# Latent attention: the reciprocal of the softmax sums is written to its PSUM bank and multiplied from there

## The reference, cut to what matters

```
q = (x @ wq).reshape(B, T, 2, 4, 128)
k_lat, v_lat = x @ wk_down, x @ wv_down          # 2 groups x 32
k, v = k_lat @ wk_up, v_lat @ wv_up
probs = softmax(mask(einsum(q, k) * 128 ** -0.5))
y = einsum(probs, v);  x = x + y @ wo
```

## Time and profile before

| what | value |
|---|---|
| time, median of 3 runs | 1840.62 us (1838.76 to 1849.7) |
| the profiled execution | 1839.44 us, of it 1837.3 us from the first to the last instruction |
| granted TensorE clock, mean | 0.911 of full speed |
| latent attention with GpSimd's additions | 1391 to 1745 us |
| the eight reciprocals, L1588 | 26.9 us |
| the eight multiplications, L1590 | 21.6 us |

### The profile page before, as it was taken

One profiled execution on the slowest core, in us unless ns is written; L12 is line 12 of the kernel. 1 busy time (PEld: TensorE's weight loads), 2 busy tenths in 40 slices (PEclk: granted clock), 3 DMA queues, 4 the chain that ended last, 5 costly groups with the idle time before them and its releaser, 6 DMA issues.

```text
span 1837.3 us, 25913 instructions
## 1 busy us (share of the span) xinstructions
PE 1579.0 (86%) x8863; PEld 801.0 (44%) x8863; DVE 1162.2 (63%) x2315; ACT 787.1 (43%) x1031; POOL 802.8 (44%) x987
## 2 busy tenths in 40 slices
PE   4666599869999999999699959998968978898779
PEld 2222366533334333343266636776634333333256
DVE  5888632489878788786243243334268988887841
ACT  2232233263565565556533324444443333444443
POOL 1223663645464636463636363500002546667900
PEclk9788599986999999999889979998988988999979
DMA  5000000141102002000000000000043000000000
GB/s 146 1 0 0 1 1 0 46 117 32 28 2 54 2 5 51 2 3 2 1 1 1 0 0 1 0 0 1 0 137 96 23 23 1 1 1 1 1 6 17
DMA packets 39123, 36.88 MB, mean 20 GB/s; under 512 B 10191, under 2 KB 36272, under 8 KB 38899
## 3 DMA queue, kind: packets, MB, share of 16 engines
q1 hardware_dynamic: 36826, 28.48, 5.5%
q10 hardware_dynamic: 2136, 7.10, 1.8%
q0 software_dynamic: 64, 0.00, 0.0%
HBM read 26.10 MB, written 8.91 MB: 19 GB/s over the span
## 4 chain that ended last, share of the span: by engine, by line
PE 68%; DVE 14%; issue 3%; ACT 3%; POOL 2%; DMA 1%; SPq 0%; DVEq 0%; POOLq 0%; ACTq 0%
PE PS L1374 11%; PE PS L948 10%; PE PS L1322 10%; PE PS L1393 10%; PE PS L936 9%; PE PS L1822 3%; PE PS L1840 3%; DVE sb_rope_mp L1558 3%; POOL sb_H L1480 2%; DVE sb_latent_mp L1558 2%; DVE sb_latent_rec L1588 1%; DVE sb_H L227 1%; PE PS L1834 1%; PE PS L941 1%; PE PS L1351 1%
## 5 line engine op out<-in xcount | busy, mean ns | idle before, releaser
L1558 DVE TENSOR_REDUCE sb_rope_mp<-PS 128x1 f32<-128x512 f32 (+3 forms) x560 | 344.3, 667 | 65.1 <-PE PS L1326 31.3
L1435 ACT ACTIVATE sb_rope_PT<-PS 128x1024 f32<-128x1024 f32 (+3 forms) x320 | 273.4, 895 | 203.8 <-PE PS L1378 104.3
L1000 DVE SCALAR_TENSOR_TENSOR sb_X<-PS,sb_gates,sb_X 128x128 f32 (+1 forms) x320 | 90.1, 344 | 241.2 <-PE PS L948 241.2
L1322 PE MATMUL PS<-sb_rope_K,sb_rope_Q 96*128 96x512 bf16 (+3 forms) x640 | 212.5, 372 | 11.7 <-ACT sb_rope_V L1420 9.6
L581 POOL TENSOR_SCALAR sb_pbelow<-sb_pa,sb_ptrial 128x512 f32<-128x512 f32 x124 | 196.8, 1597 | 6.4
L1558 DVE TENSOR_REDUCE sb_latent_mp<-PS 128x1 f32<-128x512 f32 (+2 forms) x280 | 175.5, 668 | 36.6 <-PE PS L1322 26.7
L588 POOL TENSOR_TENSOR sb_pbelow<-sb_pbelow 128x1024 f32<-128x1024 f32 (+1 forms) x248 | 182.0, 734 | 19.6
L936 PE MATMUL PS<-sb_HT,sb_w 128*128 (+1 forms) x384 | 182.0, 611 | 3.9 <-DVE sb_seed L519 2.3
L1374 PE MATMUL PS<-sb_rope_Q,sb_rope_K 99*128 99x512 bf16 (+3 forms) x640 | 179.4, 352 | 1.4 <-ACT sb_rope_PT L1435 0.9
L1374 PE MATMUL PS<-sb_latent_Q,sb_latent_K 96*128 96x512 bf16 (+7 forms) x640 | 158.8, 369 | 5.4 <-ACT sb_w0b L1435 2.4
L977 ACT ACTIVATE sb_moe_hidden<-PS,sb_vec 128x512 f32<-128x512 f32 x128 | 87.7, 687 | 159.8 <-PE PS L936 155.6
(11 more groups left out here) (315 smaller groups left out, 2716.9 us busy)
## 6 DMA issues: line engine op xcount, KB each, us to landing
sb_latent_Q<-latent_parts SPq DMA_DIRECT2D x48, 128.0 KB, 2.8
sb_rope_Q<-rope_parts ACTq DMA_DIRECT2D x9, 384.0 KB
rope_parts<-sb_rope_parts SPq DMA_DIRECT2D x24, 128.0 KB, 2.4
latent_parts<-sb_latent_parts SPq DMA_DIRECT2D x12, 256.0 KB, 2.6
sb_rope_tab<-in_rotation SPq DMA_DIRECT2D x1, 2048.0 KB, 8.2
sb_rope_K<-rope_parts ACTq DMA_DIRECT2D x6, 256.0 KB
latent_parts<-sb_latent_parts SPq DMA_DIRECT2D x12, 128.0 KB, 2.5
sb_latent_K<-latent_parts SPq DMA_DIRECT2D x48, 32.0 KB, 2.2
```

What stands on the lines that cost most here:

```text
L1000: ins = v.scalar_tensor_tensor(xi, k.PS[:, 4 + b:5 + b, i * P:(i + 1) * P], gate, xi, ALU.mult, ALU.add)
L1322: ins = pe.matmul(k.PS[:, bank, at:at + w], self.Q[0:self.rows, g % 2, j, 0, q0:q0 + P], self.K[0:self.rows, g % 2, j % self.kheads, 0, kc ...
L1435: s.activation(self.PT[u % self.B][:, 2 * p:2 * p + 2, q0:CH], k.PS[:, 2 * p:2 * p + 2, q0:CH], ACT.Exp, scale=self.scale).then_inc(self.e ...
L1558: v.tensor_reduce(self.mp[:, n % 2, kc, heads[0]:heads[-1] + 1, i], k.PS[:, bank, 0:len(heads) * w].rearrange("p (h k) -> p h k", h=len(he ...
```

## The change

Of the branch for `summed`, the reciprocal now writes to the PSUM bank it reads, and the multiplication reads the reciprocal there. Both are followed by a wait for their own end (`ch`). `normed` and `free` are raised by two separate semaphore instructions after the multiplication; before, `free` was raised by the reciprocal itself and `normed` by the multiplication. The tile `rec` isn't used in this stage any more. The additions of GpSimd and of DVE stay as they are.

```diff
                 v.wait_ge(self.moved, n + 1)
-                v.reciprocal(self.rec[:, :], k.bank(bank)).then_inc(free, 1)
-                v.wait_ge(free, uses + 1)
-                v.tensor_tensor(self.On[:, n % 2, :], self.O[:, n % 2, :], self.rec[:, :], ALU.mult) \
-                    .then_inc(self.normed, 1)
+                ch(v.reciprocal(k.bank(bank), k.bank(bank)))
+                ch(v.tensor_tensor(self.On[:, n % 2, :], self.O[:, n % 2, :], k.bank(bank), ALU.mult))
+                v.sem_inc(self.normed, 1)
+                v.sem_inc(free, 1)
             else:
                 ch(v.tensor_tensor(self.On[:, n % 2, :], self.O[:, n % 2, :], k.bank(bank), ALU.mult))
```

## The result

The changed kernel took 1835.03 us (median of 19 runs, 1823.63 to 1847.3), the kernel before, measured again with it, 1848.49 us (19 runs, 1837.35 to 1853.99). The ratio is 0.9931, with a 95% interval of 0.9909 to 0.9953: 12.8 us less, 8.7 to 16.8. The forecast was 19.5 us less, 1821 us, in a range from 1810 to 1832. The median lies above the range; the direction was right, the gain two thirds of the one forecast, and the kernel before itself measured 8 us above the 1840.62 that the forecast was taken from. Both differences are followed up here. Taken as a gain, 12.8 us does lie in what the range allows (8.6 to 30.6 us under 1840.6), at its low end.

A forecast was written before the change was run, and what follows sets the result against it. PE bound the chain (68%), waiting for a ring bank while L1590 waited for GpSimd. DVE's 17.4 us in chunks 1 to 5 plus 2.2 in chunks 6 and 7 made 19.6, taken as 19.5: 1840.6 - 19.5 = 1821 us, range 1810 to 1832.

The forecast's parts named there:

- What stretched the multiplication, and what a PSUM operand does: L1590: with two SBUF inputs it waits for GpSimd's addition; reading PSUM, 0.686 us each, DVE's sum 16.1 us less.
- The reciprocal's bound of 0.04 us: Reciprocal writing PSUM: no change expected, bounded by 0.04 us either way, 0.3 us for eight.
- Bookkeeping and the held bank: Behind each multiplication: separate semaphores cost 0.25 us; bank freed 0.94 us later, without starving DVE in chunks 1 to 6.
- The chain, 12.3 us in chunks 1 to 5: PE's waits at the sums: 17.0 us of "issue" become 5 x 0.94 = 4.7, 12.3 us gained.
- What is late next: DVE's additions L1480 behind the sums wait for GpSimd likewise, leaving DVE 1.75 us ahead per chunk, not 2.8.
- the 17.4 us: DVE's side of chunks 1 to 5: 5 x 1.75 plus 8.6 us of its idle time at low clock.
- The clock, 8 us: TensorE behind five sums: low clock falls from 33.7 to 17 us, each worth half; 8 us gained.
- Chunk 6, 2.3 us: Copy L1478 done earlier, POOL's next addition sooner: 2.5 us gained, less 0.2 for one more collision.
- the additions inherit the wait: Rival: DVE becomes the bound through its additions waiting for GpSimd; 11 us gained, 1829.6 us; chance 0.10.
- the clock falls as before: Rival: pauses of a microsecond suffice for low clock; only the chain's 14.5 us gained, 1826 us; chance 0.18.
- Slower by over 1%: Whole kernel: would need 2.3 us more per chunk, called twice what the other side costs; chance 0.02.
- the other side: Rival: multiplication still waits for GpSimd and the bank is passed on late; 4 us slower, 1844.6 us; chance 0.05.

The follow-up runs named there:

- e1: Kernel before, with the bank held until the multiplication's end and both semaphores raised separately, reciprocal still to SBUF: stage 348.7 us, before 352.0.
- e4: Changed kernel, but the multiplication itself raises the bank's semaphore and PE and ACT wait for that instead of `normed`: stage 332.4 us, changed kernel 338.6.
- e2: Kernel before, with VectorE's second-unit addition in chunks 2 to 7 replaced by a maximum with one SBUF input: stage 352.2 us, before 352.0.
- e3: Changed kernel, with VectorE's second-unit addition in chunks 2 to 7 replaced by a maximum with one SBUF input: stage 331.7 us, changed kernel 338.6.
- e11: Changed kernel, with the negated maxima kept in the last maximum's PSUM bank for the split, in both causal attentions: stage 332.5 us, ratio 0.9864 to before.
- e7: Changed kernel, with TensorE's pauses behind the sums and ahead of the maxima's transposes filled by products that change nothing: stage 324.9 us, ratio 0.9852 to before.
- e12: Changed kernel plus multiplication raising the bank's semaphore, TensorE fills, last chunk's additions on VectorE, split in PSUM: stage 307.3 us, 1793.4 us, ratio 0.9704 to before.

## Why the prediction was right or wrong

- *What stretched the multiplication, and what a PSUM operand does.* Right: 0.686 us in all eight. L1599 was the right row. The reciprocal's bound of 0.04 us held (0.009).
- *Bookkeeping and the held bank.* 0.25 us idle behind each multiplication, as in the earlier trace rows. Holding the bank is free over the stage (e1), as forecast; that the bookkeeping counts on the path is likely by e4, and not shown.
- *The chain, 12.3 us in chunks 1 to 5.* In chunk 1 TensorE's restart came 2.76 us earlier, as worked out, but the gain wasn't kept. The five intervals behind these chunks' sums gained 11.6 us with the clock's share in it.
- *What is late next, the step that failed.* The additions met GpSimd as foreseen (1.66, 1.80, 1.26, 1.14 and 1.14 us, the last three shorter than the 1.5 to 2 named as a sign), and VectorE was 1.8, 1.7, 1.8, 1.8 and 1.8 us ahead at their ends, against the 1.75 worked out. The text then let VectorE make up 8.6 us more out of its own idle time in the windows of low clock. Measured, chunks 1 to 5 gained 11.6 us against 17.4: 2.9 above the 5 x 1.75 at the additions. What happened in its place: the prolonged additions stopped TensorE a second time in all five chunks (0.64 to 1.44 us), the clock was low again behind three of them, and in these windows VectorE still stood idle for 1.55, 0.86 and 2.16 us. With the additions out of GpSimd's way, from e2 to e3, the same five intervals gained 18.0 us (with one other collision in each of the two runs, as said above). So the 17.4 us would have needed additions that don't inherit the wait, and the text had itself foreseen that they do.
- *The clock, 8 us.* Mis-sized too. Low clock behind the sums halved as assumed (33.7 to 17.0), but grew by 6.8 at the transposes, 10.2 less in all; and each is worth a third to a half and not fully half: 3.4 to 5.1 us in place of 8, an estimate. That the sum behind the five chunks came to the assumed 17.0 is luck: it was 6.8, 3.4, 0, 6.8 and 0 and not five times 3.4.
- *Chunk 6, 2.3 us.* GpSimd's gap closed and L1478 took 0.89 us; 1.62 were measured. VectorE's first three additions behind it had taken 0.69 us and now take 3.84, 3.35 and 3.28, which likely cost the rest.
- *Sum.* 13.3 = 8.2 to 9.9 of waits and 3.4 to 5.1 of clock, between the rival "the additions inherit the wait" (11) and "the clock falls as before" (14.5). The forecast of 19.5 would have needed e3's conditions (20.4 from e2 to e3).
- *The level.* A median of three runs and one profile stood for a kernel whose unchanged first stretch differs by up to 14 us from profile to profile. 0.9931 of 1840.62 is 1827.9, inside the range; the re-measured level put it outside. The 2 us left in the range for this were too few.
- *A slip beside the path.* "Slower by over 1%" needs 2.3 us more per chunk; the other side costs 0.5 us per chunk by its own sum, so that is over four times as much and not twice. The chance of 0.02 doesn't suffer by it.

## What to carry to other kernels

When one engine's instruction stretches because it waits for another's, look at all instructions of that form on the engine and not only at the longest: taking one away shifts the others into the same wait (the additions here, then a subtraction of 16 columns). Putting one input in PSUM took such instructions out of GpSimd's way at next to no price (0.009 us for the reciprocal, 0.008 for a subtraction of 16 columns, and 0.25 us idle where the semaphores are raised by separate instructions); for the smallest ones it pays where TensorE waits for them. And before a difference of 1% is forecast from a profile, cut it into stages and ask how far the unchanged ones can move.

## What the hardware showed beyond that

- A DVE cast or subtraction of 16 columns (0.174 us) can take 2.9 us beside a GpSimd addition; with its first input in PSUM it took 0.173 to 0.183 in every one of the 96 cases of e11 (four steps, 24 splits). The Trainium skill (SBUF — State Buffer, Who interferes with whom) states that copies and casts can enter a mode with both SBUF ports and then contend with GpSimd, and that an instruction with two SBUF inputs contends with its reads. The casts and the subtractions agree. The same section of the Trainium skill says that the first to start keeps the ports for its whole instruction. The trace agrees: a multiplication of VectorE that began 0.17 us after a GpSimd addition of 3.42 us took 3.80 us, and 0.69 beside none.
- 2048 columns were added by VectorE in 2.29 us, alone, against 3.2 to 3.8 us for 1536 on GpSimd and 512 on VectorE side by side.
- Behind the sums of the changed kernel TensorE's clock stayed up in chunk 5, over pauses of 1.09 and 0.78 us, and fell in chunk 4 for 6.8 us, behind a pause of 1.09 and ahead of one of 0.64; it fell in chunks 1 and 2 (1.09 and 1.18; 1.09 and 1.44) and stayed up in chunk 3 (0.85 and 0.90). The pauses' length alone doesn't tell which way it goes. In e7, with the pauses filled by products of one zero weight column, 2.8 of the stage's 324.9 us were at the low clock, and in e12 none.
